# Forward transform of sixteen images: two rows of a plane on each partition, the transform along h by quarters of the array, and spectral weights loaded between the images

## What is computed

```python
def _gn(v, G=32, eps=1e-5): ...            # group norm over pairs of channels
def spectral_conv2d(x, w1, w2):
    x_ft = jnp.fft.rfft2(x)
    out_ft[:, :, :16, :16]  = einsum('bixy,ioxy->boxy', x_ft[:, :, :16, :16], w1)
    out_ft[:, :, -16:, :16] = einsum('bixy,ioxy->boxy', x_ft[:, :, -16:, :16], w2)
    return jnp.fft.irfft2(out_ft)
y = spectral_conv2d(gn(x)) + conv1x1(gn(x)) + bias
y = kan_linear(kan_linear(y))               # two KAN layers over the channels
return x + gelu(y)
```

## Time and profile before

| what | us |
|---|---|
| median of 3 runs (3782.95 to 3789.09) | 3788.58 |
| profiled execution, its own time | 3786.73 |
| its span | 3784.9 |
| TensorE busy in the span | 3662.3 (97%) |
| VectorE busy | 3518.6 (93%) |
| ScalarE busy | 3391.7 (90%) |
| chain that ended last: TensorE's share | 87%, of it L1057 82% |

### The profile page before, as it was taken

The page is one execution under the profiler, slowest core; times in us unless marked ns, Lnnn a source line. Parts: engine busy times, 40 slices in busy tenths (PEclk is TensorE's granted clock), DMA queues, the critical chain, the costliest instruction groups (busy, mean ns, idle before and its releaser), DMA issues.

```text
span 3784.9 us, 101254 instructions
## 1 busy us (share of the span) xinstructions
PE 3662.3 (97%) x37164; PEld 2765.6 (73%) x37164; DVE 3518.6 (93%) x3900; ACT 3391.7 (90%) x3509; POOL 110.9 (3%) x132
## 2 busy tenths in 40 slices
PE   8986599999999999999999999999999999999998
PEld 4446257777777777777777777777777777777774
DVE  7762399999999999999999999999999999999996
ACT  4531399999999999999999999999999999999996
POOL 0000000000000000000000000000000000000000
PEclk9998799999999999999999999999999999999999
DMA  9997622322322322322332332332332232232232
GB/s 263 290 248 152 232 56 60 72 66 60 72 66 60 72 67 60 72 67 60 72 69 57 72 72 55 71 72 56 70 72 57 69 72 58 68 72 58 68 72 45
DMA packets 322041, 328.62 MB, mean 87 GB/s; under 512 B 86864, under 2 KB 251216, under 8 KB 319952
## 3 DMA queue, kind: packets, MB, share of 16 engines
q1 hardware_dynamic: 301008, 256.73, 25.0%
q0 software_dynamic: 18432, 67.12, 11.2%
q10 hardware_dynamic: 2560, 4.20, 0.5%
HBM read 239.88 MB, written 88.08 MB: 87 GB/s over the span
## 4 chain that ended last, share of the span: by engine, by line
PE 87%; DVE 0%; issue 0%; ACT 0%; POOL 0%; POOLq 0%; ACTq 0%; DVEq 0%
PE l_ps L1057 82%; PE y_ps L1044 3%; PE y_ps L1036 2%; DVE cube2l L933 0%; DVE cube3r L933 0%; ACT above L972 0%; ACT size L983 0%; ACT offset L987 0%; ACT S L976 0%; ACT below L980 0%; DVE cube1r L933 0%; DVE cube1l L933 0%; DVE cube0l L933 0%; ACT L976 0%; DVE cube0r L933 0%
## 5 line engine op out<-in xcount | busy, mean ns | idle before, releaser
L987 ACT ACTIVATE offset<-size 128x1024 f32<-128x1024 f32 x1280 | 1240.5, 1044 | 8.1
L933 DVE SCALAR_TENSOR_TENSOR cube0r<-below,offset 128x1024 f32<-128x1024 f32 x256 | 314.3, 1228 | 57.3 <-ACT offset L987 56.7
L1057 PE MATMUL l_ps<-S,turned_w 64*64 64x512 f32 x2048 | 330.5, 592 | 8.1 <-issue 8.1
L1057 PE MATMUL l_ps<-cube1l,turned_w 64*64 64x512 f32 x2048 | 330.0, 589 | 1.0 <-issue 1.0
L1057 PE MATMUL l_ps<-cube0r,turned_w 64*64 64x512 f32 x2048 | 329.9, 591 | 0.6 <-DVE cube0r L933 0.6
L1057 PE MATMUL l_ps<-cube3r,turned_w 64*64 64x512 f32 x2048 | 329.7, 589 | 0.8 <-DVE cube3r L933 0.8
L1057 PE MATMUL l_ps<-below,turned_w 64*64 64x512 f32 x2048 | 329.9, 591 | 0.0
L1057 PE MATMUL l_ps<-cube4r,turned_w 64*64 64x512 f32 x2048 | 329.7, 589 | 0.1
L1057 PE MATMUL l_ps<-cube4l,turned_w 64*64 64x512 f32 x2048 | 329.7, 589 | 0.1
L1057 PE MATMUL l_ps<-cube3l,turned_w 64*64 64x512 f32 x2048 | 329.7, 589 | 0.1
L1057 PE MATMUL l_ps<-cube2r,turned_w 64*64 64x512 f32 x2048 | 329.6, 589 | 0.0
(11 more groups left out here) (121 smaller groups left out, 7481.4 us busy)
## 6 DMA issues: line engine op xcount, KB each, us to landing
big<-in_x_dram SPq DMA_DIRECT2D x128, 512.0 KB, 7.0
x_ring<-in_x_dram SPq DMA_DIRECT2D x256, 256.0 KB, 4.0
act_out<-in_x_dram POOLq DMA_DIRECT2D x128, 512.0 KB, 6.8
out_dram<-act_out SPq DMA_DIRECT2D x128, 512.0 KB, 2.7
rows_scratch<-rows SPq DMA_DIRECT2D x16, 1024.0 KB, 7.0
rows_t<-rows_scratch SPq DMA_DIRECT2D x512, 32.0 KB, 5.5
big<-in_spec_w_r_dram SPq DMA_DIRECT2D x16, 512.0 KB, 11.1
big<-in_spec_w_i_dram SPq DMA_DIRECT2D x16, 512.0 KB, 11.2
```

What stands on the lines that cost most here:

```text
L933: nc.vector.scalar_tensor_tensor(out=cube[q][side][:], in0=distance[layer][:], scalar=EDGE - KNOTS[q], in1=offset[layer][q][:], op0=ALU.mi ...
L987: nc.scalar.activation(offset[layer][q][:], size[layer][:], ACT.Square, bias=-KNOTS[q]).then_inc(offset_ready[layer], 1)
L1057: ins = nc.tensor.matmul(dst[cols, r * MM:(r + 1) * MM], kan_w[layer][rows_, f, :], src[rows_, n * MM:(n + 1) * MM], start=(f == 0), stop= ...
```

## The change

It does four things.

1. An image is laid out with two rows of a plane on a partition: partition r*64 + h' holds rows 2h' and 2h'+1 of the channels with c % 2 = r. A chunk still has eight planes and 512 KB, but a contiguous piece of it is 1024 bytes (two rows of 128 float32 values), where it was 512 bytes (one row).
2. The transform along h is done by quarters of the array: `dft_h_sb` holds the table's even and odd rows on both halves of the partitions. A call of `h` now takes two chunks (16 planes) in eight matmuls of 64 rows, 64 columns and 512 elements: for each of the two rows on a partition, four quarters, the second row added to the first in PSUM. `along_h` gets four PSUM buffers, and `weights_ps` is now a view of `planes`. `image` calls `h` four times, with two turns behind each.
3. SP loads spectral weights among the images: behind each of images 2 to 9 one DMA of the imaginary part of w1 (into `big[:, 3]`), behind each of images 10 to 15 one of the real part (into `big[:, 2]`), then its last two, and then the eight of the real part of w2 into `big[:, 0]`, once images up to 14 are transformed. The block with the statistics loads only the imaginary part of w2.
4. Waits and counts follow: TensorE waits until all turned KAN weights are kept before image 1, and ScalarE writes `freq` with other strides.

```diff
+    dft_h = np.concatenate([dft_h.reshape(H // 2, 2, C)] * 2, 0)
...
-def load_mix_weights(sp, t, dst, g, part):
+def load_mix_weights(sp, t, dst, g, part, o0, half):
     src = ((t["w1_r"], t["w1_i"]), (t["w2_r"], t["w2_i"]))[g][part]
-    for o0 in range(0, C, MIX_O):
-        for half in range(2):
-            x0 = SH * (half if g == 0 else 1 - half)
-            sp.dma_start(dst[half * C:(half + 1) * C, o0:o0 + MIX_O, :, :],
-                         src[:, o0:o0 + MIX_O, x0:x0 + SH, :]).then_inc(t["mix_loaded"][g][part], 16)
+    x0 = SH * (half if g == 0 else 1 - half)
+    sp.dma_start(dst[half * C:(half + 1) * C, bass.ds(o0, MIX_O), :, :],
+                 src[:, bass.ds(o0, MIX_O), x0:x0 + SH, :]).then_inc(t["mix_loaded"][g][part], 16)
...
-        along_h = [ctx.enter_context(nc.psum_tensor(f"along_h{i}", [P, HALF, W], F32)) for i in range(2)]
+        along_h = [ctx.enter_context(nc.psum_tensor(f"along_h{i}", [P, HALF, W], F32)) for i in range(4)]
...
-                src = t["x"][b].rearrange("c h w -> h c w") if isinstance(b, int) else \
-                    t["x"][bass.ds(b, 1)].rearrange("a c h w -> h (a c) w")
-                sp.dma_start(img[:, par, chunk(k), :], src[:, chunk(k), :]).then_inc(img_loaded[par][k], 16)
+                src = t["x"][bass.ds(b, 1)].rearrange("a (g r) (h t) w -> (r h) (a g) (t w)", r=2, t=2)
+                sp.dma_start(img[:, par, chunk(k), :, :].rearrange("p g t w -> p g (t w)"),
+                             src[:, chunk(k), :]).then_inc(img_loaded[par][k], 16)
...
-            with sp.Fori(1, B // 2) as b2:
+            def next_image(b2, par):
+                for k in range(N_GRP):
+                    sp.wait_ge(along_h_done, N_GRP * b2 + (N_GRP // 2 * (par - 2) + k // 2 + 1))
...
+                    load(par, 2 * b2 + par, k)
+            with sp.Fori(1, 5) as b2:
                 for par in range(2):
...
+                    next_image(b2, par)
+                    load_mix_weights(sp, t, weights[:, 3], 0, 1, MIX_O * b2 - MIX_O, par)
             sp.wait_ge(consts_loaded, 112)
-            load_mix_weights(sp, t, weights[:, 2], 0, 0)
+            sp.wait_ge(weights_turned, len(TURNS))
+            with sp.Fori(5, B // 2) as b2:
+                for par in range(2):
+                    next_image(b2, par)
+                    load_mix_weights(sp, t, weights[:, 2], 0, 0, MIX_O * b2 - 5 * MIX_O, par)
+            for half in range(2):
+                load_mix_weights(sp, t, weights[:, 2], 0, 0, C - MIX_O, half)
+            sp.wait_ge(along_h_done, N_GRP // 2 * (B - 1))
+            sp.wait_ge(stats_ready, N_GRP * (B - 1))
+            for o0 in range(0, C, MIX_O):
+                for half in range(2):
+                    load_mix_weights(sp, t, weights[:, 0], 1, 0, o0, half)
...
             def h(b, b2, par, k):
-                pe.wait_ge(img_loaded[par][k], 16 * (b2 + 1))
-                pe.wait_ge(flat_ready, N_GRP * b + (k + 1))
...
+                for q in range(2):
+                    pe.wait_ge(img_loaded[par][2 * k + q], 16 * (b2 + 1))
+                pe.wait_ge(flat_ready, N_GRP * b + (2 * k + 2))
+                pe.sem_inc(seen_by_pe, 1)
+                for rows2 in range(2):
+                    for q in range(2):
+                        for r in range(2):
+                            own = slice(r * C, (r + 1) * C)
+                            ins = nc.tensor.matmul(along_h[2 * (k % 2) + r][q * C:(q + 1) * C, :, :],
+                                                   dft_h_sb[own, rows2, :], img[own, par, chunk(2 * k + q), rows2, :],
+                                                   start=(rows2 == 0), stop=(rows2 == 1), skip_group_check=True,
+                                                   tile_position=(r * C, q * C))
                 ins.then_inc(along_h_done, 1)
...
+            pe.wait_ge(weights_kept, len(TURNS))
...
-            for g, part in ((0, 1), (1, 0), (1, 1)):
-                load_mix_weights(sp, t, mix_w[g][part], g, part)
+            for o0 in range(0, C, MIX_O):
+                for half in range(2):
+                    load_mix_weights(sp, t, mix_w[1][1], 1, 1, o0, half)
```

More of the change, by code:

```diff
@@ L277, in forward @@
         freq = sb("freq", [P, 2, NU, C])
-        dft_h_sb = sb("dft_h_sb", [P, C])
+        dft_h_sb = sb("dft_h_sb", [P, 2, C])
         dft_w_sb = sb("dft_w_sb", [P, 2, 4 * MODES])
         eye = sb("eye_all", [P, P])
-        along_h = [ctx.enter_context(nc.psum_tensor(f"along_h{i}", [P, HALF, W], F32)) for i in range(2)]
+        along_h = [ctx.enter_context(nc.psum_tensor(f"along_h{i}", [P, HALF, W], F32)) for i in range(4)]
         turned = [ctx.enter_context(nc.psum_tensor(f"planes{i}", [P, HALF, P], F32)) for i in range(2)]
         along_w = ctx.enter_context(nc.psum_tensor("along_w", [P, PLACES, 2, 2 * MODES], F32))
-        weights_ps = [ctx.enter_context(nc.psum_tensor(f"weights_ps{i}", [P, 4, 2, C], F32)) for i in range(2)]
+        weights_ps = [turned[i][:].rearrange("p f (l o) -> p f l o", l=2) for i in range(2)]
         TURNS = [(f, min(f + 4, NF + 1)) for f in range(0, NF + 1, 4)]
@@ L332, in _ @@
                                  kan["bias"][l * C:(l + 1) * C]).then_inc(consts_loaded, 16)
-            with sp.Fori(1, B // 2) as b2:
-                for par in range(2):
[L335 to L341, removed]
-            sp.wait_ge(consts_loaded, 112)
-            load_mix_weights(sp, t, weights[:, 2], 0, 0)
+            def next_image(b2, par):
+                for k in range(N_GRP):
+                    sp.wait_ge(along_h_done, N_GRP * b2 + (N_GRP // 2 * (par - 2) + k // 2 + 1))
+                    sp.sem_inc(seen_by_sp, 1)
+                    sp.wait_ge(stats_ready, 2 * N_GRP * b2 + (N_GRP * (par - 2) + k + 1))
+                    sp.sem_inc(seen_by_sp, 1)
+                    load(par, 2 * b2 + par, k)
+            with sp.Fori(1, 5) as b2:
+                for par in range(2):
+                    next_image(b2, par)
+                    load_mix_weights(sp, t, weights[:, 3], 0, 1, MIX_O * b2 - MIX_O, par)
+            sp.wait_ge(consts_loaded, 112)
+            sp.wait_ge(weights_turned, len(TURNS))
[10 more added lines that the diff above has]
+                    load_mix_weights(sp, t, weights[:, 0], 1, 0, o0, half)
         @block.vector
@@ L381, in h @@
             def h(b, b2, par, k):
-                pe.wait_ge(img_loaded[par][k], 16 * (b2 + 1))
-                pe.wait_ge(flat_ready, N_GRP * b + (k + 1))
[L384 to L388, removed]
+                for q in range(2):
[10 more added lines that the diff above has]
+                                                   tile_position=(r * C, q * C))
                 ins.then_inc(along_h_done, 1)
             def turn(b, k):
-                pe.wait_ge(flat_ready, N_GRP * b + (k + 3))
+                pe.wait_ge(flat_ready, N_GRP * b + (k + 5))
                 pe.wait_ge(freq_ready, N_GRP * b + (k + 1))
@@ L414, in image @@
                 h(b, b2, par, 0)
-                for k in range(1, N_GRP):
+                for k in range(1, N_GRP // 2):
                     h(b, b2, par, k)
-                    turn(b, k - 1)
+                    turn(b, 2 * k - 2)
+                    turn(b, 2 * k - 1)
                 if before:
                     w(b - 1, 1 - par)
+                turn(b, N_GRP - 2)
                 turn(b, N_GRP - 1)
@@ L454, in order @@
                 act.wait_ge(along_w_done, b + 1)
-                dst = freq[:, par, :, chunk(k)].rearrange("w u (g c) -> w u g c", g=2)
-                src = turned[k % 2][:].rearrange("w c (g u) -> w u g c", g=2)[:, 0:NU]
+                dst = freq[:, par, :, :].rearrange("w u (k q g r) -> w k r u q g", q=2, g=HALF, r=2)[:, k // 2, k % 2]
+                src = turned[k % 2][:].rearrange("w g (q u) -> w u q g", q=2)[:, 0:NU]
                 nc.scalar.activation(dst, src, ACT.Copy).then_inc(freq_ready, 1)
```

15 lines of the change are left out of this document (8 added, 7 removed).

## The result

The changed kernel takes 3796.16 us, the median of 10 runs (3794.45 to 3799.98); the kernel before takes 3787.02 in the runs beside it. The ratio is 1.0025, interval 1.0017 to 1.0033: slower by 9 us, where the forecast of 3770 is 17 us less. The profiled execution took 3797.01 us with a span of 3795.2.

A forecast was written before the change was run, and what follows sets the result against it. Image loop bound by TensorE with DMA close behind, mixing by weight loads. Barrier at 264.5, inverse_rows at 350.7 instead of 368.98: 18.3 us less, 3786.7 to 3768.4, plus 1.85 for the median, so 3770; range 3757 to 3787.

The forecast's parts named there:

- I take the first eight as measured (19.67) and the rest at 2.69: Weight DMAs ahead of the barrier: 24 instead of 8, 19.67 + 16 x 2.69 = 62.7 us.
- SP's list: SP's DMA issues up to the barrier: loads, 112 chunks, 24 weight DMAs; done at 263.9 us instead of 258.9.
- Both ends, 2.37 and 3.05 us: Range for the cost of one weight DMA in SP's list, from measured rows: 18.98 / 8 to 24.43 / 8.
- 1 KB pieces: Image chunk DMAs: pieces grow from 512 to 1024 bytes, giving 352 GB/s, 1.488 us a chunk instead of 1.786.
- the new wait: Barrier after the images: it waits for SP, lets go at 264.5 us, with the chain of the statistics behind it.
- Quarters: TensorE's transform along h: a group of eight matmuls at full rate costs 2 x 0.86 + 0.15 = 1.87 us.
- TensorE's side at 254.1: TensorE's work would let the barrier go at 254.1 us, hidden under SP's 263.9 with 9.8 us to spare.
- No change: Rival, chance 0.10: smaller fixed packet part, or weight DMAs at 3.05 us among the images; leaves 3781 to 3796.
- The slower rival: Packet size does not matter, chance 0.07: chunks stay at 1.786 us, images and barrier wait for DMA; 3808.
- image starts lie 17 us apart: Sign in the image loop that the forecast is wrong, with GB/s staying at 290; forecast 14.5 to 14.7 us.
- GB/s at 290: Sign in the queues, 100 to 230 us, that the forecast is wrong; forecast well over 290, near 350.

The follow-up runs named there:

- experiments 3: Changed kernel, its 14 weight DMAs in the loop reading with output channel on the partitions (1 KB apart, not 64 KB), writes the same; 3796.16 us.
- 4: Changed kernel, its 14 weight DMAs in the loop writing all 128 partitions, read from the image tensor, same bytes; 3757.97 us.
- experiment 5: Changed kernel, its 14 weight DMAs in the loop writing every other partition instead of 64 adjacent ones, same source and pieces; 3754.71 us.
- experiment 1: Changed kernel with the weights back behind the images (eight before the barrier, 24 behind), so layout and quarters alone; 3770.05 us.
- experiment 2: Kernel before the change with only the weight DMAs moved among the images, old layout and 512-byte pieces; 3819.28 us.
- experiment 11: Changed layout and quarters, 13 weight DMAs behind the images before the barrier; ScalarE's queue issues w2's second halves while SP issues the first; 3764.50 us.

## Why the prediction was wrong

**The step that failed** is "I take the first eight as measured (19.67) and the rest at 2.69", in SP's list, for the DMAs that stand among images. The list, in its own terms: 33.15 + 112 x 1.50 less 3.1 for the first eight chunks + 13 x 4.9 + 30.65 for the last 11 = 292.4 (measured 292.3). The images and the start differ from the forecast by 3 us together. The 24 weight DMAs take 94 us instead of 62.7, against the forecast's mean of 2.61 each: 13 of them 30 more, the last 11 (2.79 each) 2 more. That 31 us, less the 3 gained, is the list's 28.4 us, and with 22.9 instead of 23.1 to the mixing, 61.7 instead of 63.1 from there to inverse_rows, and 1.8 more in the rest, the miss of 28.6 us in the profiled execution (26 in the medians).

**Why the bounds didn't hold it.** Both ends, 2.37 and 3.05 us, were rows of weights among weights. No row of the trace had a weight DMA between images, and I carried the price over as if a DMA's cost were its own. What it does to its neighbours is part of it: the rate stays down for ten us. Shown is that the side-by-side half of the partitions does this (experiments 3, 4, 5). The packets of the change's trace show the neighbours: from 132 to 135 us, where weights and chunks are under way together, a 1 KB packet of a chunk takes 128 ns in the median, against 48 with images alone (126 to 131 us), and both together move as little as 124 GB/s in one us. With every other partition (experiment 5) a chunk's packets beside weights take 52 ns. Why the two together fall below the 175 GB/s of one half alone, and so why a weight DMA costs 4.9 us among images and 3.0 alone, stays open.

**What was right.** 1 KB pieces gave 347 to 350 GB/s (forecast 352). The barrier waited for SP, the new wait that I had named. The mixing started 22.9 us behind it with no wait for weights. Quarters ran at full rate: 1.88 us a group for 1.87. A gain of that size was in reach, though not by the forecast's way: layout and quarters alone gave 17, where the forecast counted on earlier weights as well.

**Sizes that were off.** An image of TensorE takes 13.7 us, not 14.45, since two turns in a row take 1.02, not 1.18, four times in an image, and two groups in a row 3.59 (experiment 1) in place of 3.74. Experiment 1 shows it as 243.4 for the barrier where the forecast had TensorE's side at 254.1; in the change it didn't count, as the loads were the bound.

**The rivals.** "No change" held the mechanism, weights dearer among images, but ended at 3.05 us. The slower rival named the place, a barrier that waits behind loads moved ahead of the statistics, with another cause: packets, which did gain. Its test, "image starts lie 17 us apart", came out (16.9) for the wrong reason, while its other sign, GB/s at 290, came out as 283 from valleys and peaks, and a mean over 130 us could not tell them apart; single slices could. The Trainium skill's 512 bytes for line rate (DMA: Bandwidth & Descriptors, Specifications) don't fit what was measured: 290 GB/s at 512 bytes, 347 at 1 KB. No run took the size of the pieces apart from the new order of the reads.

**Left open:** from inverse_rows to the end the changed kernel takes 3417.7 us, before 3415.9. The kernels of the other runs with the new layout show 0.6 to 3.8 more and that of experiment 2 shows 1.2 less, in blocks that the change doesn't touch. Each is one execution, and ten of the kernel before spread over 7 us (3782.01 to 3789.09), so no cause can be read from it.

## What to carry to other kernels

Price a DMA by the partitions that it writes and by what is in the queues beside it: a transfer to 64 partitions side by side costs most where another stream needs the rate. Two queues that write different halves at a time reach the full rate (experiment 11), though that kernel lost more elsewhere than it gained by it. Put such loads where nobody waits, here the stretch in which SP stood idle ahead of a barrier, and count what the barrier waits for. A busy share of 1 in the DMA engines says nothing of how much they move; read the GB/s beside it, in slices short enough to show a single transfer.

## What the runs showed of the hardware

- 512 KB in 512-byte pieces: to 64 partitions side by side 3.0 us (175 GB/s) for one half over and over, 2.6 to 2.7 (193 to 202) with halves in turns, 1.8 to 2.0 (290) to every other partition; 4.9 among chunks that write all partitions in 1.50 us.
- The DMA share reads 1.21 at 193 GB/s and 1.10 at 347: at the slow rate the engines look busier, not idler.
- TensorE's granted clock was 0.52 in the stretch of the wait from 138 to 142 us and 0.63 in the next, 1.2 GHz for the most of both; ahead of it TensorE had stood for 3.75 us. A late chunk costs its wait and then slower matmuls.
- Two hardware queues, SP's and ScalarE's: 176 GB/s with both on the same half, 273 to 290 with one half each. GpSimd's queue beside SP's took six times SP's bytes from 250 to 270 us.
- Beside packets to one half, a 1 KB packet to any partition takes 128 ns in the median instead of 48; beside packets to every other partition 52.
